# Routed expert tiles with their weights fetched from DRAM as the stationary side, eight exponential buffers, paired weighted sums

## The chip, the cores and the metric

One core of one Trainium2 chip runs the whole program. The metric is device time of one launch in microseconds; where several runs were made, their median counts.

## The reference

The input x has 8 batches of 512 tokens, width 128, float32. Two layers follow each other. In each, for every batch:

```python
h = layernorm(x) * (1 + ca) + sa
x = x + ga * attention(h)          # 16 heads of 8, softmax over 512 keys (causal in layer 1)
h = layernorm(x) * (1 + cb) + sb
x = x + gb * ffn(h)
```

The feed-forward part of layer 0 is a mixture of 8 experts, of which each token takes its best 2, plus a shared expert of width 192; an expert is `(silu(t @ w1) * (t @ w3)) @ w2` with a hidden width of 352. The feed-forward part of layer 1 has 8 experts of width 128 with a squared relu, also with the best 2 per token, and attention there makes q, k and v by way of a latent of 32. The factors sa, ca, ga, sb, cb, gb come from a small product per batch.

## The kernel before, in words

An *item* i is a batch in a layer: items 0 to 7 are layer 0 (`NB` = 8), items 8 to 15 (`N` = 16) layer 1. All matrix work in float32 but the scores (bf16 in three parts) is done as two TensorE instructions per product, which stand as two MATMUL rows in the profile.

**The order of work** is not written by hand. `plan()` (L167) lists some thousands of units of work by `add(engine, key, weight, urgency, after, ...)`, and `Plan.settle` (L92) simulates the five engines with these weights and lags: each engine takes, among the units that can start within `SLACK` (L156) of the earliest, the one of lowest urgency. Urgency is the item's number plus an offset in items, shifted by family in `SHIFT`, and for layer 1 and the last three items in `LATE` and `LAST` (L57 to L61). What comes out is one fixed list per engine (`todo`) and the PSUM banks of each unit. The engines then run their lists in order, each with semaphore waits for what a unit needs. SP's list holds nearly all DMAs, POOL's the indirect ones, so a unit of SP that waits holds up every DMA listed behind it. TensorE has three modes for the plan: "half" (scores, two row halves of the array), "cols" (`pv`, four column groups) and "full" (everything else); a change of mode is given 0.1 us.

**Attention.** For an item and half f of its heads, `score` (L639) makes 128 queries x 512 keys of two heads at a time in two PSUM banks (L647), and `rowmax` (L875) on VectorE takes the maxima; 32 of each per item. The maxima are turned (`max_turn`), split (`max_hi`, `max_lo`), stored to DRAM (`max_st`, L1508) and loaded as three more rows of the query operand (`max_ld`, L1513). `bscore` (L668) then makes keys x queries with the maximum already taken off, `expo` (L1226, ScalarE) writes the exponentials of two heads into one of `NES` = 6 buffers `ES`, and `pv` (L685) sums the values weighted by them: one `pv` per group g of four heads and per key tile j of 128 keys, of four matmuls of 9 columns x 512, one in each column group. A `pv` needs the two `expo` of its j; with six buffers three j are in flight, and `expo` waits for the `pv` of three key tiles before. `u_copy`, `u_st`, `u_ld`, `t_rc`, `t_st`, `t_ld`, `t_o`, `t_mm` (L695) carry the sums through DRAM to the output projection. Each item is begun about one period ahead by `p_norm` (L1161), `p_turn`, `p_ht`, `p_proj` (L630), `p_v`. The buffers `hP` and `lat` are the buffer `xn[0]` (L450), so `p_norm` of an item waits for `p_v` and `p_proj` of the item before.

**Routed experts of layer 0.** For each pair of batches q (items 2q and 2q+1) the 2048 token slots are sorted by expert: `rr_mm`, `rr_a`, `rr_pos`, `rr_tex` find each slot's place and each tile's expert, `r_sc` (L1391, POOL, 16 indirect DMAs, two in flight) scatters rows to `d_h`. There are `NMT` = 23 tiles of 128 rows per pair, 92 in all, and `NXL` = 6 loads of four tiles: `x_ld` (L1564) into the one buffer `hs`, `x_turn` (L743) and `x_hst` make them width x rows in `hsT`. A tile j is then:

- `x_up` (L752), twice: stationary the tile of `hsT` (128 x 128), moving 352 columns of the expert's w1 or w3. All experts' weights lie in SBUF (`f1`, `f3`, `f2`, loaded once); the columns are found by a register, `bass.ds(v, 352)`. Result rows x hidden.
- `x_th` (L1261), `x_gate` (L1061), `x_mul` (L1068): the gated product `hdx`, 128 x 352.
- `x_ht` (L759): three transposes; `x_hc` (L1267): a ScalarE copy to `hxT`.
- `x_dn` (L769): three matmuls of 128 columns, one bank, against rows of `f2` found by a register.
- `x_y` (L1276) and, per four tiles, `x_st` (L1569) to `d_y`.

The registers are loaded on TensorE's own sequencer by `x_reg` (L731), twice per pair, 24 registers each. `x_up` also waits for a `score` of the item that `SPREAD` names, which spaces the tiles out. When a pair's `x_st` are done, `g_ga` (L1414, POOL, indirect) gathers for each 128 tokens two sets of rows into `gr` (four buffers, so a gather waits for the `g_w` of two token tiles before), `g_w` (L1078, L1082) weights them, `g_x` adds them to x. Item 8 + b of layer 1 starts after `g_x` of item b.

**Layer 1's experts** are dense: `d_up` (L777), `d_relu`, `d_sq`, `d_dn` (L784: four matmuls of a new 128 x 128 stationary tile and 128 moving columns each), `d_y`, `d_add` per expert.

Of the kernel before, what the change touches and what calls it, by code (L numbers as in the profile page):

```python
# [17 lines left out]
E = 8  # L18
NG = H // 4
NSTK = 4  # L20
NES = 6
# [35 lines left out]
SHIFT = {"t": -0.39, "s": 1.02, "p": -0.35, "stack": -0.35, "pv": 0.11, "f": 0.37, "d": 1.41, "x": 1.14, "max": -0.38, "r": 0.28, "rr": 0.28, "u": -0.15, "g": -0.54, "bscore": -0.08, "expo": -0.08}  # L57


LATE = {"d": -0.05, "f": -0.22, "score": 0.12, "rowmax": 0.12, "t": 0.43, "max": 0.24, "g": 0.09, "u": 0.82}  # L60
LAST = {"max": -0.08, "r": -0.06, "rr": -0.06, "pv": 0.15}  # L61


class Plan:
# [8 lines left out]
    def add(self, engine, key, weight, urgency, after=(), lag=None, mode="full", opens=0, closes=()):  # L73
# [7 lines left out]
        self.work[key] = (engine, weight, urgency, after, lag, mode, opens, closes)  # L81
# [74 lines left out]
SLACK, SWITCH = 0.05, 0.1  # L156

SPREAD = 2.4, 1.8
# [3 lines left out]
def after_t(i):  # L162

    return ("t_rv" if T_ON_DVE[i] else "t_res", i)


def plan():  # L167
# [17 lines left out]
    for n, name in enumerate(("bo", "c1", "f1s", "f3s", "f2s")):  # L185
# [3 lines left out]
    load("f1", 2.0, 8.0, after=[("score", 2, 0, 0, 0)])  # L189
    load("f3", 2.3, 8.0, after=[("score", 2, 0, 3, 0)])  # L190
    load("f2", 2.6, 8.0, after=[("score", 2, 1, 0, 0)])
# [21 lines left out]
    for i in range(N):  # L213
# [5 lines left out]
        add("ACT", ("p_norm", i), 0.9, i - 0.1, [("p_rstd", i), ("p_turn", i - 1)] + [("p_v", i - 1), ("p_proj", i - 1, 0), ("p_proj", i - 1, 1)])  # L219
        add("PE", ("p_turn", i), 0.45, i, [("p_norm", i), ("c_pool",), ("m_one", l), ("p_v", i - 1), ("p_proj", i - 1, 1), ("p_lat", i - 1)], opens=1)  # L220
        add("ACT", ("p_ht", i), 0.67, i, [("p_turn", i), ("m_one", l), ("p_v", i - 1), ("p_lat", i - 1)], closes=[("p_turn", i)])
        x = ("p_ht", i)
        if not big:
            add("PE", ("p_lat", i), 0.95, i, [("p_ht", i), ("ld", "w1"), ("p_v", i - 1)], opens=1)
            add("ACT", ("p_latc", i), 0.49, i, [("p_lat", i), ("p_v", i - 1)], closes=[("p_lat", i)])
            x = ("p_latc", i)
# [34 lines left out]
        for g in range(NG):  # L261
            f = g // 2
            for j in range(NT):
                u = i + 1.0 + 0.25 * g + 0.0625 * j
                n = S if big else S - 128 * j
                m = NT * (NG * i + g) + j - 3
# [7 lines left out]
                add("PE", ("pv", i, g, j), 0.12 + 0.86 * n / 512, u + 0.06, exps[-2:] + [("p_vs", i)] + ([("pv", i, g, j - 1)] if j else []), mode="cols", opens=int(j == 0))  # L274
# [8 lines left out]
            if i < N - 1 else [("x_up", NB // 2 - 1, NMT - 1, 1)]), lag=4.0)  # L283
# [124 lines left out]
def program(nc, xin, cT, wm, w0, wf1, wf3, wf2, w1, wr1, wr2, bo, out):  # L408
    ctx = ExitStack()
    with ctx:  # L410
# [132 lines left out]
        for n in range(4):  # L543
            s["g_ga", n] = ctx.enter_context(nc.semaphore(f"g_ga{n}"))
# [1100 lines left out]
```

## Time and profile before

| | us |
|---|---|
| median of 3 runs | 1226.88 |
| the runs | 1226.86, 1226.88, 1234.54 |
| the profiled execution | 1231.06 |
| its span, first to last instruction | 1229.0 |

In the rows below, "PE" is TensorE's matmuls, "PEld" its weight loads, "DVE" VectorE, "ACT" ScalarE, "POOL" GpSimd, "SPq" the DMA issues of SP. Times are us unless marked ns; L752 is line 752 of the kernel. On a busy TensorE the distance from one row's start to the next row's start is what the first one cost; the printed duration of a row runs on into the next, since matmuls overlap.

### The profile page before, as it was taken

The numbers are of one execution on the slowest core, as the hardware profiler recorded it, in microseconds if no ns is written. First come the engines' busy times: TensorE is split into PE (matmuls) and PEld (weight loads), VectorE is DVE, ScalarE is ACT, GpSimd is POOL, SyncE is SP. The second block draws the span as 40 slices with busy tenths as digits, with TensorE's granted clock in tenths as the row PEclk, the third lists the DMA queues.
The fourth block names the chain that finished last, engine by engine and source line by source line (L and its number), as shares of the span: only waits on it lengthen the run. The fifth ranks groups of instructions, "written<-read, shape, count | busy, mean of one in ns | idle before, by whom it ended". The sixth has DMA issues, their size and how long they took to land.

```text
span 1229.0 us, 22171 instructions
## 1 busy us (share of the span) xinstructions
PE 1089.1 (89%) x7912; PEld 504.0 (41%) x7912; DVE 879.4 (72%) x1813; ACT 775.3 (63%) x1327; POOL 408.9 (33%) x462
## 2 busy tenths in 40 slices
PE   5588798889999898999989998989998999999985
PEld 3122222123444343444544545545554444544453
DVE  5899788878887676786657776667565777777354
ACT  3058577567766666568765665646766576776853
POOL 2000204250205326314246242351115652433352
PEclk8579898889999898999998999989998899999998
DMA  4705472533316125116144162451512615431110
GB/s 115 167 31 139 175 188 73 138 107 110 101 58 176 50 87 126 62 63 149 60 124 98 36 169 68 112 124 39 132 52 80 149 56 124 113 84 39 55 37 17
DMA packets 120699, 119.36 MB, mean 97 GB/s; under 512 B 17856, under 2 KB 102592, under 8 KB 120208
## 3 DMA queue, kind: packets, MB, share of 16 engines
q1 hardware_dynamic: 115280, 106.68, 32.7%
q0 software_dynamic: 4736, 10.49, 3.0%
q8 instruction: 64, 1.05, 0.4%
q10 hardware_dynamic: 576, 0.79, 0.2%
q14 instruction: 43, 0.35, 0.1%
HBM read 59.26 MB, written 58.62 MB: 96 GB/s over the span
## 4 chain that ended last, share of the span: by engine, by line
PE 47%; DMA 15%; DVE 13%; issue 9%; ACT 8%; POOL 5%; SPq 1%; POOLq 0%; ACTq 0%; DVEq 0%
PE ps L685 9%; PE ps L752 6%; DMA gr<-d_y,pos 6%; DVE nm L875 6%; PE ps L647 5%; PE ps L668 5%; PE ps L769 3%; ACT ES L1226 3%; PE ps L784 3%; DMA d_h<-hx,pos 3%; PE ps L777 2%; ACT xn L1161 2%; PE ps L713 2%; PE ps L759 2%; DMA d_u<-US 2%
## 5 line engine op out<-in xcount | busy, mean ns | idle before, releaser
L875 DVE TENSOR_REDUCE nm<-ps 128x2 f32<-128x1024 f32 (+3 forms) x512 | 508.7, 1018 | 110.9 <-PE ps L653 58.2
L1226 ACT ACTIVATE ES<-ps 128x1024 f32<-128x1024 f32 (+3 forms) x512 | 432.4, 864 | 172.5 <-PE ps L668 94.0
L685 PE MATMUL ps<-ES,VS 128*9 128x512 f32 (+3 forms) x2048 | 237.2, 539 | 1.1 <-DVE nmp L886 0.5
L647 PE MATMUL ps<-KS,QS 48*128 48x512 bf16 (+3 forms) x1024 | 185.6, 369 | 46.8 <-DVE nm L875 26.0
L668 PE MATMUL ps<-QS,KS 51*128 51x512 bf16 (+3 forms) x1024 | 179.9, 355 | 15.1 <-DVE nm L875 5.7
L752 PE MATMUL ps<-f,hsT 128*128 x368 | 142.5, 491 | 5.8 <-DVE nm L875 3.3
L647 PEld LDWEIGHTS ps<-KS,QS 48*128 48x128 bf16 x1024 | 50.5, 95 | 193.6 <-issue 64.3
L668 PEld LDWEIGHTS ps<-QS,KS 51*128 51x128 bf16 x1024 | 49.9, 95 | 177.7 <-issue 73.3
L1434 POOL TENSOR_TENSOR ya<-ya,yS 128x512 f32<-128x512 f32 x49 | 62.2, 1269 | 155.1 <-DVE yS L1121 154.9
L1355 POOL TENSOR_TENSOR sp<-sr,sp 128x512 bf16<-128x512 f32 x32 | 37.1, 1158 | 199.8 <-ACT sp L1202 199.5
L1391 POOL DMA_INDIRECT d_h<-hx,pos x64 | 63.2, 988 | 89.4 <-DMA d_h<-hx,pos 52.1
L1414 POOL DMA_INDIRECT gr<-d_y,pos x64 | 66.6, 1040 | 63.3 <-DMA gr<-d_y,pos 26.1
L769 PE MATMUL ps<-f,hxT 128*128 x552 | 85.5, 292 | 0.9 <-DVE hdx L1061 0.6
L769 PEld LDWEIGHTS ps<-f,hxT 128*128 128x128 f32 x552 | 72.5, 196 | 32.2 <-issue 28.7
L784 PE MATMUL ps<-r,hd 128*128 128x128 f32 x512 | 73.5, 290 | 6.4 <-ACT hd L1298 2.4
L752 PEld LDWEIGHTS ps<-f,hsT 128*128 128x128 f32 x368 | 61.2, 195 | 43.0 <-issue 33.1
L1061 DVE SCALAR_TENSOR_TENSOR hdx<-tx,ps 128x352 f32<-128x352 f32 x92 | 47.2, 514 | 38.4 <-ACT tx L1261 34.6
L784 PEld LDWEIGHTS ps<-r,hd 128*128 128x128 f32 x512 | 64.2, 197 | 24.1 <-ACT hd L1298 13.3
L1290 ACT ACTIVATE tt<-ps 128x512 f32<-128x512 f32 x64 | 38.0, 595 | 45.7 <-PE ps L777 43.7
L777 PE MATMUL ps<-hF,r 128*128 128x512 f32 x112 | 61.7, 634 | 1.9 <-DVE ya L1114 1.7
L1161 ACT ACTIVATE xn<-X,rs 128x128 f32<-128x128 f32 x128 | 52.5, 483 | 16.6 <-POOL rs L1351 16.5
L685 PEld LDWEIGHTS ps<-ES,VS 128*9 128x9 f32 x2048 | 31.3, 89 | 74.4 <-issue 61.0
(190 smaller groups left out, 1471.7 us busy)
## 6 DMA issues: line engine op xcount, KB each, us to landing
d_u<-US SPq DMA_DIRECT2D x64, 256.0 KB
KS<-d_k SPq DMA_DIRECT2D x64, 192.0 KB
QS<-d_q SPq DMA_DIRECT2D x64, 192.0 KB
d_q<-sp SPq DMA_DIRECT2D x16, 384.0 KB
d_k<-sp SPq DMA_DIRECT2D x16, 384.0 KB
hs<-d_h SPq DMA_DIRECT2D x20, 256.0 KB
d_y<-ys SPq DMA_DIRECT2D x20, 256.0 KB, 2.3
d_q<-sp SPq DMA_DIRECT2D x16, 256.0 KB
```

What stands on the lines that cost most here:

```text
L647: mm = eng.matmul(psum[:, bank[u][a], 0:n], QS[m][r:r + KA, pr, 128 * t:128 * t + 128], KS[m][r:r + KA, pr, 0:n], start=True, stop=i < NB)
L668: mm = eng.matmul(psum[:, bank[u][a], 0:S - q0], KS[m][r:r + KB, pr, 128 * j:128 * j + 128], QS[m][r:r + KB, pr, q0:S], start=True, stop=i ...
L685: mm = eng.matmul(psum[32 * a:32 * a + 9, b, q0:S], VS[i % 3][:, j, 4 * g + a, :], ES[(2 * (NT * (NG * i + g) + j) + a // 2) % NES][:, a % ...
L752: eng.matmul(ps(*u)[:, 0:352], T_[:, a0:a0 + 128], (f1, f3)[c][:, bass.ds(v, 352)], start=True, stop=True).then_inc(s["x_up"], 1)
L769: mm = eng.matmul(ps(*u)[:, 0:128], hxT[(NMT * p + j) % 2][0:w, 128 * n:128 * n + 128], f2v[0:w, bass.ds(v + 128 * n, 128)], start=(n == 0 ...
L777: eng.matmul(ps(*u), r1[:, e, :], hFs[i], start=True, stop=True).then_inc(s["d_up"], 1)
L784: mm = eng.matmul(ps(*u)[:, 128 * t:128 * t + 128], hd[e % 2][:, 128 * t:128 * t + 128], r2[:, e, :], start=True, stop=True)
L875: eng.tensor_reduce(nm[f][:, :].rearrange("p (a c) -> p a c", a=2)[:, :, 4 * pr + t], ps2("score", i, f, pr, t)[:, :, 0:n], AX.X, ALU.max, ...
L1161: ins = eng.activation(xn[w][:, t, :], X[:, NT * b + t, :], ACT.Identity, bias=rs[:, w, 2, t:t + 1], scale=rs[:, w, 1, t:t + 1])
L1226: eng.activation(ES[(2 * n + pp) % NES][:, :, 0:S - q0], ps2("bscore", i, f, g, j, pp)[:, :, 0:S - q0], ACT.Exp, scale=SC1 if i >= NB else ...
L1391: eng.indirect_dma_start(out=d_h[p % 2][:, :], out_offset=bass.IndirectOffsetOnAxis(ap=pos[p % 2][:, c, t8:t8 + 1], axis=0), in_=hx[t8 // ...
L1414: eng.indirect_dma_start(out=gr[m][:, :], out_offset=None, in_=d_y[p][:, :], in_offset=bass.IndirectOffsetOnAxis(ap=pos[p % 2][:, c, t8:t8 ...
```

## The change

- `NES` 6 to 8. `pv` units are planned in pairs: at odd j, after the four `expo` of j-1 and j, the `pv` of j-1 and of j are added with one urgency. `expo` waits for the `pv` of four key tiles before.
- The routed weights stay in DRAM as `we`, one block of 128 x 3 x 384 floats per expert (w1, w3 and w2 padded from 352 to 384). A unit of SP, `x_w`, loads one block of 576 KB per tile into one of `NST` = 4 buffers `wst`; it waits for `x_dn` of four tiles before. `x_reg` moves from TensorE to SP and loads 12 registers.
- `x_up` takes 128 columns of the weights as the stationary side, three times per matrix, with the tile of `hsT` as 128 moving columns. Its result is hidden x rows, so `x_ht` and `x_hc` go, `x_th`, `x_gate`, `x_mul` work on 384 columns, and `x_dn` takes `hdx` as it is.
- `hs` gets two buffers, `gr` eight, `hP` and `lat` their own; `f1`, `f2`, `f3` and their loads go, the shared expert has `fs` and one load.
- The last item's private tiles lie in `wst[0]` and `wst[1]` and wait for the last `x_dn` that used these.
- `SHIFT`, `LATE`, `LAST`, `SLACK`, `SPREAD` have other values.

```diff
-NES = 6
+NES = 8
+NST = 4
-SHIFT = {... "d": 1.41, ...}
+SHIFT = {... "d": 1.2, ...}
-LATE = {"d": -0.05, "f": -0.22, "score": 0.12, "rowmax": 0.12, "t": 0.43, "max": 0.24, "g": 0.09, "u": 0.82}
-LAST = {"max": -0.08, "r": -0.06, "rr": -0.06, "pv": 0.15}
+LATE = {... "u": 0.82, "pv": -0.02, "r": -0.23, "rr": -0.23}
+LAST = {"max": -0.08, "r": 0.47, "rr": 0.47, "pv": 0.15, "p": -0.09, "stack": -0.09, "d": 0.41, "u": 0.33, "bscore": 0.11, "expo": 0.11}
-SLACK, SWITCH = 0.05, 0.1
-SPREAD = 2.4, 1.8
+SLACK, SWITCH = 0.01, 0.1
+SPREAD = 2.2, 1.6
...
-                add("PE", ("pv", i, g, j), ..., u + 0.06, exps[-2:] + ..., mode="cols", opens=int(j == 0))
+                for j in (j - 1, j) if j % 2 else ():
+                    n = S if big else S - 128 * j
+                    add("PE", ("pv", i, g, j), ..., u + 0.06, exps[-4:] + ..., mode="cols", opens=int(j == 0))
...
-                        add("PE", ("x_reg", q, h), 2.0, u, [("rr_tex", q), ("x_dn", ...)])
+                        add("SP", ("x_reg", q, h), 1.0, u - 0.35, [("rr_tex", q), ("x_w", ...)], lag=0.1)
...
+                    n = NMT * q + j - NST
+                    add("SP", ("x_w", q, j), 0.5, u - 0.3, [("x_reg", q, h), ("x_dn", n // NMT, n % NMT)], lag=3.6)
-                    add("PE", ("x_ht", q, j), 0.34, ...)
-                    add("ACT", ("x_hc", q, j), 0.37, ...)
...
                 elif k == "x_up":
-                    v = eng.snap(rows[j % 12], min_val=0, max_val=7 * 352)
-                    eng.matmul(ps(*u)[:, 0:352], T_[:, a0:a0 + 128], (f1, f3)[c][:, bass.ds(v, 352)],
-                               start=True, stop=True).then_inc(s["x_up"], 1)
+                    for n in range(3):
+                        mm = eng.matmul(ps(*u)[:, 128 * n:128 * n + 128], wst[(NMT * p + j) % NST][:, c, 128 * n:128 * n + 128],
+                                        T_[:, a0:a0 + 128], start=True, stop=True)
+                    mm.then_inc(s["x_up"], 1)
                 elif k == "x_dn":
-                    for n, w in enumerate((128, 128, 96)):
-                        v = eng.snap(cols[j % 12], min_val=0, max_val=7 * 384)
-                        mm = eng.matmul(ps(*u)[:, 0:128], hxT[...][0:w, 128 * n:128 * n + 128],
-                                        f2v[0:w, bass.ds(v + 128 * n, 128)], start=(n == 0), stop=(n == 2))
+                    for n in range(3):
+                        mm = eng.matmul(ps(*u)[:, 0:128], hdx[...][:, 128 * n:128 * n + 128],
+                                        wst[...][:, 2, 128 * n:128 * n + 128], start=(n == 0), stop=(n == 2))
...
+                elif k == "x_w":
+                    if NMT * p + j >= NST:
+                        q.wait_ge(*on("x_dn", *tile_before(p, j, NST)))
+                    v = eng.snap(tiles[j % 12], min_val=0, max_val=7 * 128)
+                    eng.dma_start(wst[(NMT * p + j) % NST][:, :, :].rearrange("p a b -> p (a b)"),
+                                  we[bass.ds(v, 128), :]).then_inc(slot(*u), 16)
```

## Rows read from the trace of the kernel before

**Rows 1.** The page: the span, and busy time of each engine.
```profile
span 1229.0 us, 22171 instructions
PE 1089.1 (89%) x7912; PEld 504.0 (41%) x7912; DVE 879.4 (72%) x1813; ACT 775.3 (63%) x1327; POOL 408.9 (33%) x462
```

**Rows 2.** Four stretches: length, busy us (count) of each engine, PEclk, DMA share, GB/s.
```profile
60.00:280.00 220.00, 183.07 (x1113) 53.04 (x1111) 185.22 (x312) 149.88 (x198) 56.24 (x67) 0.87 0.43 121
280.00:930.00 650.00, 608.01 (x4366) 300.56 (x4365) 458.02 (x972) 422.73 (x763) 212.96 (x228) 0.97 0.35 94
930.00:1180.00 250.00, 235.51 (x2178) 116.54 (x2177) 169.64 (x395) 171.34 (x310) 111.63 (x112) 0.97 0.33 87
1180.00:1229.00 49.00, 30.50 (x159) 20.91 (x158) 23.90 (x75) 19.04 (x34) 16.48 (x17) 0.90 0.07 22
```

**Rows 3.** Groups by line: busy us, mean ns of one, idle before.
```profile
L752 PE MATMUL ps<-f,hsT 128*128 x368 | 142.5, 491 | 5.8 <-DVE nm L875 3.3 <-DVE sr L868 0.8 <-ACT US L1233 0.5
L769 PEld LDWEIGHTS ps<-f,hxT 128*128 128x128 f32 x552 | 72.5, 196 | 32.2 <-issue 28.7
L1267 ACT ACTIVATE hxT<-ps 128x384 f32<-128x384 f32 x92 | 45.1, 490 | 20.8 <-PE ps L759 20.5
```

**Rows 4.** TensorE in order of time, 572 to 577: start, us, what.
```profile
572.16 0.38 PE L668 MATMUL ps<-QS,KS 51*128 51x512 bf16 x2
572.47 1.04 PE L685 MATMUL ps<-ES,VS 128*9 128x512 f32 x8
573.45 0.39 PE L647 MATMUL ps<-KS,QS 48*128 48x512 bf16 x2
573.77 0.55 PE L759 MATMUL ps<-ident,hdx 128*128 128x128 f32 x3
574.25 0.39 PE L668 MATMUL ps<-QS,KS 51*128 51x512 bf16 x2
574.48 0.38 PE L647 MATMUL ps<-KS,QS 48*128 48x512 bf16 x2
574.79 0.86 PE L752 MATMUL ps<-f,hsT 128*128 x2
575.49 0.83 PE L769 MATMUL ps<-f,hxT 128*128 x6
576.25 0.39 PE L668 MATMUL ps<-QS,KS 51*128 51x512 bf16 x2
```

**Rows 5.** TensorE in order of time: dense experts' L784, eight products in a row.
```profile
1184.82 1.95 PE L784 MATMUL ps<-r,hd 128*128 128x128 f32 x16
1186.61 1.88 PE L777 MATMUL ps<-hF,r 128*128 128x512 f32 x4
```

**Rows 6.** TensorE in order of time: two `pv` in a row.
```profile
510.69 1.90 PE L685 MATMUL ps<-ES,VS 128*9 128x512 f32 x16
512.52 0.39 PE L647 MATMUL ps<-KS,QS 48*128 48x512 bf16 x2
```

**Rows 7.** `pv` alone in 280 to 930: PE busy, PEld busy.
```profile
280.00:930.00 650.00, 118.87 (x1024) 15.83 (x1024) 0.97 0.35 94
```

**Rows 8.** TensorE in order of time: the longest gap released by "issue".
```profile
451.47 0.39 PE L647 MATMUL ps<-KS,QS 48*128 48x512 bf16 x2 [2.06 <-issue]
```

**Rows 9.** Around 124 to 139: SP's issues, the chain that ended last, TensorE.
```profile
123.97 1.06 SPq L1466 DMA_DIRECT2D f<-wf  x2
126.34 7.91 DMA d_m<-nmp
138.80 0.58 PE L695 MATMUL ps<-w0s,OT 128*128 128x128 f32 x1 [4.85 <-DVE OT L897]
```

**Rows 10.** The page's DMA issues: count, KB each, us to landing.
```profile
f<-wf SPq DMA_DIRECT2D x2, 1408.0 KB, 7.3
d_m<-nmp SPq DMA_DIRECT2D x32, 24.0 KB, 1.5
```

**Rows 11.** What SP's queue waited for: us, times, longest.
```profile
SPq L1564 <- PE ps L743: 80.8, 16, 12.9
```

More of the change, by code:

```diff
@@ L80, in add @@
             urgency += LAST.get(family, 0.0)
-        self.work[key] = (engine, weight, urgency, after, lag, mode, opens, closes)
+        self.work[key] = (engine, weight, round(urgency, 3), after, lag, mode, opens, closes)
     @staticmethod
@@ L164, in after_t, with last_in @@
     return ("t_rv" if T_ON_DVE[i] else "t_res", i)
+def last_in(m):
+    n = max(n for n in range(NB // 2 * NMT) if n % NST == m)
+    return n // NMT, n % NMT
 def plan():
@@ L282, in plan @@
         add("SP", ("t_gt", i), 0.5, u - 0.5, [("m_st", l)] + ([("s_x", i - 2), ("r_hx", i - 2), after_t(i - 2), ("d_x", i - 2)]
-            if i < N - 1 else [("x_up", NB // 2 - 1, NMT - 1, 1)]), lag=4.0)
+            if i < N - 1 else [("x_dn", *last_in(0))]), lag=4.0)
         add("DVE", ("t_o", i), 0.61, u, [("t_ld", i)])
@@ L334, in plan @@
                     if j % 12 == 0:
-                        add("PE", ("x_reg", q, h), 2.0, u, [("rr_tex", q), ("x_dn", q - (h == 0), NMT - 1 if h == 0 else 11)])
+                        add("SP", ("x_reg", q, h), 1.0, u - 0.35, [("rr_tex", q), ("x_w", q - (h == 0), NMT - 1 if h == 0 else 11)], lag=0.1)
                     L = j // 4
@@ L376, in plan @@
             u = i + 2.35
-            add("DVE", ("d_comb", i), 0.43, u, [("f_idx", i), ("d_y", i - 2, E - 1) if i < N - 1 else ("x_dn", NB // 2 - 1, NMT - 1)])
+            add("DVE", ("d_comb", i), 0.43, u, [("f_idx", i), ("d_y", i - 2, E - 1) if i < N - 1 else ("x_dn", *last_in(1))])
             for e in range(E):
@@ L456, in program @@
         hx = [sb(f"hx{i}", [128, NT, D]) for i in range(2)]
-        hs = sb("hs", [128, 4, D])
+        hs = [sb(f"hs{i}", [128, 4, D]) for i in range(2)]
         ys = [sb(f"ys{i}", [128, 4, D]) for i in range(2)]
@@ L460, in program @@
         cv = sb("cv", [128, NT, D])
-        gr = [sb(f"gr{i}", [128, D]) for i in range(4)]
+        gr = [sb(f"gr{i}", [128, D]) for i in range(8)]
         ohs = sb("ohs", [128, 2, 8, E])
@@ L579, in _ @@
             q = Queue(eng)
-            rows, cols = ([eng.alloc_register(f"row{k}_{n}") for n in range(12)] for k in range(2))
-            f2v = f2[:, :, :].rearrange("p a b -> p (a b)")
             def open_banks(u):
@@ L1059, in _ @@
                     if p or j > 1:
-                        q.wait_ge(*on("x_ht", *tile_before(p, j, 2)))
-                    eng.scalar_tensor_tensor(out=hdx[m][:, :], in0=tx[m][:, :], scalar=1.0, in1=ps("x_up", p, j, 0)[:, 0:352],
+                        q.wait_ge(*on("x_dn", *tile_before(p, j, 2)))
+                    eng.scalar_tensor_tensor(out=hdx[m][:, :], in0=tx[m][:, :], scalar=1.0, in1=ps("x_up", p, j, 0)[:, 0:384],
                                              op0=ALU.add, op1=ALU.mult).then_inc(s[k], 1)
@@ L1151, in _ @@
                         q.wait_ge(*on(("p_turn", "f_turn")[w], i - 1))
-                    if w == 0 and i:
-                        q.wait_ge(*on("p_v", i - 1))
-                        for n in range(2):
-                            q.wait_ge(*on("p_proj", i - 1, n))
                     if w == 1 and 0 < i <= NB:
@@ L1534, in _ @@
                     if i == N - 1:
-                        q.wait_ge(*on("x_up", NB // 2 - 1, NMT - 1, 1))
+                        q.wait_ge(*on("x_dn", *last_in(0)))
                     elif i >= 2:
```

205 lines of the change are left out of this document (91 added, 114 removed).

## The prediction

> **What bounds the kernel now.** I read the page first, then busy time by stretch, then the groups by line, and last TensorE in order of time. The page gives TensorE 1089.1 of 1229.0 us, VectorE 879.4, ScalarE 775.3 [rows 1]. The stretches show that this share is not one thing [rows 2]. From 60 to 280 us, where no expert tile runs, VectorE (185.2 of 220) and TensorE (183.1, at a granted clock of 0.87) are equally full and neither sets the pace alone. From 280 to 930, where all 92 tiles lie, TensorE is busy 608.0 of 650 us (93.5%) at 0.97 of its clock, VectorE 70%, ScalarE 65%: TensorE is the bound there, and only 42 us are left over. From 930 to 1180 it is the same (235.5 of 250). The last 49 us are one item's chain, where TensorE works 30.5 us. DMA is busy 35% in the middle stretch and is not a bound, but it is what the change loads most.
>
> So the sum goes by TensorE's time from 280 to 1180, and I ask of each edit what it takes from TensorE's list there.
>
> **Tiles with the weights as the stationary side.** A busy TensorE's cost is the distance between starts. An `x_up` costs 575.49 - 574.79 = 0.70 us [rows 4], the three transposes of `x_ht` 0.48, `x_dn` 0.76. A tile before is 2 x 0.70 + 0.48 + 0.76 = 2.64 us. Afterwards `x_up` is three products of a new 128 x 128 stationary tile and 128 moving columns, which is the form of `x_dn`: 0.76. A tile is 3 x 0.76 = 2.28. The check is the dense experts' L784, of the same form, eight products in 1.79 us or 0.224 each [rows 5]; three of them and one entry of 0.09 make 0.76. The saving is 0.36 x 92 = 33 us. Units that stand directly behind each other save the entry already, so it can be less (0.24 a tile, 22 us); a visit less between two scores saves another 0.09 (rows 4: `bscore` costs 0.23 ahead of a score, 0.31 ahead of other work), at most 41. I take 30.
>
> A rule speaks against this part. The rows first: a weight load of this form lasts 0.196 us [rows 3], and a tile goes from 13 loads (4 for `x_up`, 3, 6) to 18. Rows 5 hold 16 loads, some 3.1 us of them, in 1.79 us, so they lie beside the matmuls. The Trainium skill, page "TensorE: Matmul & The Clock Gate", section "Part 3: Packing small matmuls — row/col tiling", says that a weight load overlaps running matmuls only where the row group differs, and here it is the same; by it the added loads would be exposed. The rows contradict that for this form. What exposure would cost is a rival below.
>
> **What else leaves the tile.** `x_hc` is 45.1 us of ScalarE [rows 3]; wider `x_th`, `x_gate`, `x_mul` (384 for 352 columns) give back some 3 us on ScalarE and 7 us on VectorE, neither of them the bound. The tile's own chain is shorter by about a microsecond, which matters only to the gathers behind it. I count nothing. Bounds: 7 us lost if VectorE were the bound, 5 gained.
>
> **`x_reg` to SP.** TensorE's sequencer loads 24 registers eight times. It shows as a gap released by "issue", the longest 2.06 us [rows 8]. 8 x 2.06 = 16 us; where TensorE waits anyway it is free. I take 13. On SP it is 12 loads, beside DMAs that mostly wait for something else.
>
> **Pairs of `pv`.** A lone `pv` costs 0.98 us and makes the score ahead of it 0.31 instead of 0.23 [rows 4]. Two in a row cost 1.83 [rows 6]. A merge saves 2 x 0.98 - 1.83 + 0.08 = 0.21 us. 128 of the 256 `pv` lie in the middle stretch (1024 matmuls, eight each) [rows 7]: 64 merges, 13 us, less the few that are merged already. The other 64 merges are worth another 13, half of them before 280, where TensorE isn't alone. I take 12 + 8 = 20. The wait it adds: a `pv` of an even j stands behind two more `expo`; scores and tiles of other items are queued around it, and eight buffers keep two pairs in flight, one filled while one is summed. If ScalarE then had to wait for the pair, every pair could lose up to one `expo`, 1.02 us; I see no reason in a stretch where ScalarE is 65% busy, and take nothing (bound: 10 us lost).
>
> **The loads of f1, f2, f3 go.** At 123.97 two of them are issued, 1408 KB each, and the small store of the maxima at 126.34 lands 7.91 us later instead of 1.5; TensorE then stands 4.85 us [rows 9, 10]. This gap goes: 5 us. Next is whatever VectorE and TensorE share there.
>
> **The weight blocks, `x_w`.** 92 blocks of 576 KB. In rows 9 the store behind 2816 KB came 6.4 us late, so those 2816 KB were through about 8.8 us after their issue: 1.8 us a block. That is 166 us of all DMA engines, 27% of the stretch on top of 35%. A block is wanted every 6.5 to 7 us and four are in flight, so the tile itself will rarely wait. The price is paid by others: whatever stands behind a block in SP's queue comes up to 1.8 us late, on average 0.27 x 0.9 = 0.25 us if blocks and others mix at random. Some 8 transfers in a row carry one item's attention (store of q and k, stack, maxima out and in, sums out and in, reciprocals out and in), nine items in the stretch: 72 x 0.25 = 18 us, and a third of it seen, 6 us. Lower end 0, upper end is the rival below.
>
> **SP's list.** `x_w` and `x_reg` also put 100 units into SP's in-order list, and each `x_w` waits for an `x_dn`. Behind it stand the stores of the maxima and sums, for which `bscore` and `t_mm` wait. Against this the two `hs` buffers take away most of the 80.8 us that SP stood for `x_turn` in 16 waits, up to 12.9 us long [rows 11]. I set these against each other, zero, between 15 gained and 30 lost.
>
> **Small edits.** Own `hP` and `lat`, eight `gr`: waits on work long done, or off the path, 0 to 4 us, taken as 0. The new offsets: those for `r` and `rr` in `LATE` and `LAST` touch nothing, since these units exist for items 0 to 7 alone; the rest reorders layer 1 and the last three items. `SPREAD` ends the tiles 0.4 of an item earlier. No row prices an order; TensorE's idle time after 930 is 14.5 + 18.5 us [rows 2], so I allow 12 either way and take 0.
>
> **Sum.** 30 + 13 + 20 + 5 = 68 us off TensorE's list. Not all of it becomes time: in the middle TensorE's 93.5% goes to some 91%, because waits for VectorE, ScalarE and DMA don't shrink with it. I count 0.7 of it, 48, less 6 for contention: 42 us. The profiled execution was 1231.06 (span 1229.0 and 2.1 around it), 4.2 above the median of the runs; I take the difference from the median: 1226.9 - 42 = 1185 us.
>
> **Rivals.**
> - *The whole of it and more*: TensorE takes all 68 us, and the earlier tiles and the new order add some 8. 1227 - 76 = 1151 us. For it: 93.5% busy over 650 us. Against it: the waits named. Chance 0.2.
> - *Another engine or a latency is the bound already*: the freed time of TensorE turns into waiting for VectorE's maxima and for the chain through DRAM. 1227, plus or minus 10. For it: the stretch before 280 is shared [rows 2], and 185 of 220 for VectorE is no slack. Against it: 458 of 650 for VectorE in the middle. Chance 0.13.
> - *The blocks delay everything behind them* (the slower side): each of the 72 transfers stands behind one whole block, 1.8 us, and 4.85 of 6.4 us of delay reach TensorE, as in rows 9: 72 x 1.8 x 0.76 = 98 us, against 48: 1277 us. It decides from a mean delay of 48 / (72 x 0.76) = 0.9 us a transfer, half a block. For it: one queue carries nearly all DMAs, and blocks are freed in bursts as the tiles run. Against it: the plan knows of one unit per block and keeps four buffers. Chance 0.12.
> - *Weight loads exposed*: 5 x 0.196 x 92 = 90 us against 48: 1269 us. Rows 5 speak against it. It is what the rule named above would give. Chance 0.03.
> - That a merge doesn't happen is hardly possible, since both `pv` become ready together with one urgency; if half of them are split, 10 us are lost, inside the forecast's range.
>
> **How the numbers follow.** My forecast, 1185 with its own range of 1167 to 1205, has 0.52. A measurement of this kernel tells about 1% from no change. Faster by over 1% holds the forecast and the first rival, 0.72; within 1%, 0.13; slower, 0.15. The range goes from 1148 to 1250: it leaves out part of the first rival and most of the two slow ones.
>
> **What would show it.** Right: L759 and L1267 gone; L752 as 1104 rows of the form and mean of L769 (0.275 us), about 1.4 us a tile; `pv` in runs of 16; TensorE's time from the first to the last tile down from 650 to some 605 us and its share still above 0.9; DMA share in that stretch near 0.6; landing of the small stores below 3 us. Wrong: TensorE's share below 0.88 there with VectorE or "DMA d_m", "DMA QS", "DMA DR" as releasers (contention), SP waiting long on L769 with maxima behind it, or starts of L784 and L752 more than 0.3 us apart (exposed loads). If the first item's stretch before 280 doesn't shorten at all, that takes some 8 us from my sum.

## The result and the profile after

The changed kernel takes 1249.5 us (median of 4 runs, 1244.5 to 1252.9), beside 1227.9 us for the kernel before on the same chip (4 runs, 1226.9 to 1234.5): a ratio of 1.0156, 95% interval 1.0121 to 1.0191. It is 22 us slower, where the forecast was 42 us faster. The profiled execution took 1252.24 us, with a span of 1250.5.

Busy times from the page of the changed kernel, then busy times by stretch (length, busy us and count of each engine, PEclk, DMA share, GB/s):

```profile
span 1250.5 us, 22791 instructions
PE 1068.2 (85%) x8372; PEld 548.1 (44%) x8372; DVE 882.0 (71%) x1809; ACT 742.8 (59%) x1235; POOL 409.3 (33%) x462
```

```profile
60.00:280.00 220.00, 181.79 (x1128) 52.22 (x1128) 188.20 (x321) 152.37 (x201) 56.47 (x67) 0.90 0.43 115
280.00:960.00 680.00, 599.88 (x4819) 352.16 (x4819) 456.82 (x971) 390.74 (x674) 218.78 (x235) 0.93 0.58 166
960.00:1200.00 240.00, 225.26 (x2149) 109.93 (x2147) 169.82 (x383) 167.07 (x301) 103.44 (x103) 0.99 0.33 87
```

TensorE's busy time fell, but by much less than the 68 us of the forecast: 1089.1 to 1068.2 us, by 20.9 [rows 1]. Its idle time grew by twice that: 1229.0 - 1089.1 = 139.9 us before, 1250.5 - 1068.2 = 182.3 after. Nearly all of this growth, 38 of 42 us, lies in the stretch of the tiles: TensorE is busy 88% there and was at 93.5%, the granted clock is 0.93 and was 0.97, and the DMA share is 0.58 where it was 0.35 [rows 2]. The first tile starts at 283 us, 6 us later than before. From there to the end of the last tile it takes 682 us, where it took 653 and 605 were forecast. What follows the last tile is 13 us shorter.

The groups by line (busy us, mean ns of one, idle before and its releasers), the tile's two products and their weight loads:

```profile
L750 PE MATMUL ps<-hsT,wst 128*128 128x128 f32 x1104 | 162.9, 294 | 6.6 <-DVE hdx L1048 2.7 <-DVE nm L864 1.9 <-DVE hd L964 1.1
L750 PEld LDWEIGHTS ps<-hsT,wst 128*128 128x128 f32 x1104 | 142.8, 202 | 41.5 <-issue 31.7 <-DVE hdx L1048 4.8 <-DVE nm L864 2.0
L758 PE MATMUL ps<-wst,hdx 128*128 128x128 f32 x552 | 87.5, 297 | 13.0 <-DVE hdx L1055 12.6 <-ACT US L1219 0.4
```

And of the kernel before the two that stood beside L752 of [rows 3]:

```profile
L769 PE MATMUL ps<-f,hxT 128*128 x552 | 85.5, 292 | 0.9 <-DVE hdx L1061 0.6
L759 PE MATMUL ps<-ident,hdx 128*128 128x128 f32 (+1 forms) x276 | 49.2, 288 | 3.4 <-DVE hdx L1068 3.3
```

The tiles cost 142.5 + 49.2 + 85.5 = 277.2 us before and 162.9 + 87.5 = 250.4 after. 27 us are gone, and the loads of the stationary side (142.8 us of them for `x_up`) lie beside the products. The whole of TensorE agrees: busy time times the mean granted clock, a measure of the work that doesn't move with the clock, is 1089.1 x 0.933 = 1016 us before and 1068.2 x 0.926 = 989 after, 27 less. So only the tiles' part of the forecast shows in TensorE's work (`x_reg` and the loads of f were gaps), and a lower clock gives back 6 us of it.

Where the waits are, from the profile's list of waits (engine, line, releaser: total us, times, longest):

```profile
POOL d_h L1371 <- DMA d_h<-hx,pos: 71.0, 25, 7.4
POOL gr L1394 <- DMA gr<-d_y,pos: 50.1, 22, 5.4
PE ps L651 <- DVE nm L864: 44.0, 39, 9.0
PE ps L672 <- DVE nm L864: 23.2, 21, 5.6
PE ps L672 <- ACT ES L1212: 16.0, 9, 13.0
DVE DC L881 <- DMA OT<-d_u: 33.2, 9, 11.0
ACT xn L1144 <- POOL rs L1331: 30.0, 14, 13.4
```

and the same of the kernel before:

```profile
POOL d_h L1391 <- DMA d_h<-hx,pos: 52.1, 26, 5.5
POOL gr L1414 <- DMA gr<-d_y,pos: 26.1, 17, 3.4
PE ps L647 <- DVE nm L875: 26.0, 34, 3.0
PE ps L668 <- DVE nm L875: 5.7, 13, 1.3
ACT xn L1161 <- POOL rs L1351: 16.5, 11, 3.8
```

The waits for DMA rose on GpSimd, and each engine's wait for the next rose behind it. One case in full, in order of time (start, us, what, idle before and releaser), is TensorE's longest gap:

```profile
405.07 0.97 POOL L1371 DMA_INDIRECT d_h<-hx,pos  x1 [3.40 <-DMA d_h<-hx,pos]
408.57 0.97 POOL L1371 DMA_INDIRECT d_h<-hx,pos  x1 [1.25 <-DMA d_h<-hx,pos]
410.89 0.23 POOL L1326 TENSOR_SCALAR rs<-mv 128x4 f32<-128x4 f32 x1
412.86 1.65 ACT L1144 ACTIVATE xn<-X,rs 128x128 f32<-128x128 f32 x4 [13.43 <-POOL rs L1331]
414.41 1.00 ACT L1212 ACTIVATE ES<-ps 128x1024 f32<-128x1024 f32 x1
415.47 0.61 PE L672 MATMUL ps<-QS,KS 51*128 51x512 bf16 x2 [12.96 <-ACT ES L1212]
```

GpSimd scatters rows to DRAM, two transfers in flight, and each next one waits for the landing of the one two before. `rs`, four short operations of the next item's norm, stands in its list behind them; six are issued while ScalarE waits. ScalarE's `p_norm` waits for `rs` for 13.4 us, an `expo` stands behind `p_norm`, and TensorE stands 13 us for the `expo`.

### The profile page after: what moved, and what is told of

It reads as the page before. It is cut to its first block, busy times and chain, and to the rows that moved or that the text cites. A ratio compares the mean times of both kernels' runs of the same rounds, so it can differ in the third digit from the quotient of the medians.

```text
span 1250.5 us, 22791 instructions
## 1 busy us (share of the span) xinstructions
PE 1068.2 (85%) x8372; PEld 548.1 (44%) x8372; DVE 882.0 (71%) x1809; ACT 742.8 (59%) x1235; POOL 409.3 (33%) x462
## 4 chain that ended last, share of the span: by engine, by line
PE 34%; DMA 22%; issue 14%; DVE 13%; POOL 8%; ACT 6%; SPq 1%; POOLq 0%; DVEq 0%; ACTq 0%
DMA d_h<-hx,pos 9%; DMA gr<-d_y,pos 8%; PE ps L689 7%; DVE nm L864 6%; PE ps L750 5%; PE ps L672 4%; PE ps L651 3%; PE ps L758 3%; PE ps L773 3%; ACT xn L1144 2%; POOL gr L1394 2%; ACT ES L1212 2%; PE ps L766 2%; POOL d_h L1371 2%; PE ps L717 1%
## 5 line engine op out<-in xcount | busy, mean ns | idle before, releaser
L864 DVE TENSOR_REDUCE nm<-ps 128x2 f32<-128x1024 f32 (+3 forms) x512 | 507.2, 1016 | 109.8 <-PE ps L657 57.3
L689 PE MATMUL ps<-ES,VS 128*9 128x512 f32 (+3 forms) x2048 | 237.8, 539 | 0.3 <-DVE rj L990 0.2
L750 PE MATMUL ps<-hsT,wst 128*128 128x128 f32 x1104 | 162.9, 294 | 6.6 <-DVE hdx L1048 2.7
L750 PEld LDWEIGHTS ps<-hsT,wst 128*128 128x128 f32 x1104 | 142.8, 202 | 41.5 <-issue 31.7
L758 PE MATMUL ps<-wst,hdx 128*128 128x128 f32 x552 | 87.5, 297 | 13.0 <-DVE hdx L1055 12.6
L758 PEld LDWEIGHTS ps<-wst,hdx 128*128 128x128 f32 x552 | 72.8, 200 | 33.9 <-DVE hdx L1055 16.1
L1048 DVE SCALAR_TENSOR_TENSOR hdx<-tx,ps 128x384 f32<-128x384 f32 x92 | 50.3, 546 | 34.3 <-ACT tx L1247 33.9
L773 PEld LDWEIGHTS ps<-r,hd 128*128 128x128 f32 x512 | 61.6, 191 | 24.2 <-ACT hd L1278 14.5
L1247 ACT ACTIVATE tx<-ps 128x384 f32<-128x384 f32 x92 | 45.2, 491 | 37.3 <-PE ps L750 31.2
L689 PEld LDWEIGHTS ps<-ES,VS 128*9 128x9 f32 x2048 | 31.0, 89 | 69.1 <-issue 58.9
```

The source lines that it names most:

```text
L689: mm = eng.matmul(psum[32 * a:32 * a + 9, b, q0:S], VS[i % 3][:, j, 4 * g + a, :], ES[(2 * (NT * (NG * i + g) + j) + a // 2) % NES][:, a % ...
L750: mm = eng.matmul(ps(*u)[:, 128 * n:128 * n + 128], wst[(NMT * p + j) % NST][:, c, 128 * n:128 * n + 128], T_[:, a0:a0 + 128], start=True, ...
L758: mm = eng.matmul(ps(*u)[:, 0:128], hdx[(NMT * p + j) % 2][:, 128 * n:128 * n + 128], wst[(NMT * p + j) % NST][:, 2, 128 * n:128 * n + 128 ...
L773: mm = eng.matmul(ps(*u)[:, 128 * t:128 * t + 128], hd[e % 2][:, 128 * t:128 * t + 128], r2[:, e, :], start=True, stop=True)
L864: eng.tensor_reduce(nm[f][:, :].rearrange("p (a c) -> p a c", a=2)[:, :, 4 * pr + t], ps2("score", i, f, pr, t)[:, :, 0:n], AX.X, ALU.max, ...
```

## The experiments

Theory A: the weight blocks (576 KB each, 54 MB in all) make other transfers land late, and this is what costs. Theory B: the new order of the lists costs. Theory C: the pairs of `pv` cost. All ratios are to the kernel before, with 95% intervals.

**The blocks without most of their bytes.** Every engine's list stays as it is. 88 of the 92 blocks bring 64 KB in place of 576, 46 of the 54 MB are gone, and the later tiles compute with what stood in their buffers:

```diff
-                    eng.dma_start(wst[...], we[bass.ds(v, 128), :])
+                    cut = 3 * 384 if NMT * p + j < NST else 128
+                    eng.dma_start(wst[...][:, 0:cut], we[bass.ds(v, 128), 0:cut])
```

> The kernel after the change, every list and wait as it is; only the first four weight blocks are loaded whole, the other 88 bring 128 of 1152 columns (64 instead of 576 KB), so later tiles compute with stale weights. Theory 1 (the bytes of the blocks lengthen the serial indirect DMAs, 16 scatters from 34.3 us to 39.8 and 16 gathers from 36.9 to 41.0 on average, and POOL, VectorE, SP and ScalarE stand behind them in their fixed lists): the chains go back to under 37 us, TensorE's gaps of 5 to 13 us go, and the time falls by 20 us or more, to 1229 or less. Theory 2 (the new order of the lists itself, with SP's waits for x_dn, costs the time): within 6 us of the 1249.5 of the changed kernel.

1206.1 us (0.9805, 0.9751 to 0.9859). The bytes cost 1249.5 - 1206.1 = 43 us, and without them the change would gain 21. SyncE's time for the 92 issues is not part of it: about 34 us in both traces. The gap of 12.96 us shown above is 7.8 us here.

**The kernel before with the traffic alone**: 92 transfers of 576 KB from DRAM to DRAM, issued from SyncE between the first `x_ld` and the last `x_st` of each pair of items; nobody waits for them.

```diff
+                for n in extra.get(u, ()):
+                    eng.dma_start(d_s[n], wx).then_inc(more, 16)
```

> The kernel before, its lists untouched, with 92 more DMAs in SP's list that nobody waits for: 576 KB each, 23 of them spaced evenly over the units from a pair's first x_ld to its last x_st, from DRAM to DRAM in rows of 4608 bytes. It keeps the old tiles, six buffers and the old constants. Theory 1 (bytes beside the indirect DMAs): slower than before by 20 us or more, 1248 and up, with TensorE's gaps of several us before work that a late scatter or gather holds up. Theory 2 (the order of the lists): within 8 us of 1228, since SP's issue of 92 DMAs is some 35 us in a queue that mostly waits.

1280.8 us (1.041, 1.0352 to 1.0468): 53 us for 54 MB that are read and also written to DRAM. Two kernels with unlike lists pay a price of the same size. This run alone doesn't part the bytes from the 92 issues, which take SyncE some 0.51 us each; the run before does.

**The pairs of `pv` made one unit.** A `pv` is eight MATMUL instructions. In TensorE's order of time, 246 rows of L689 hold eight and only 5 hold sixteen (238 and 9 in the kernel before): the planner did not put the two of a pair one behind the other. Here it must:

```diff
-                for j in (j - 1, j) if j % 2 else ():
-                    n = S if big else S - 128 * j
+                if j % 2:
+                    n = 2 * S if big else 2 * (S - 128 * j) + 128
```

> The kernel after the change, with the pv of two key tiles as one unit of the plan, so that they stand directly behind each other; in the changed kernel they don't (226 pieces of 8 matmuls in the trace, 5 of 16), because the second of a pair is given the lag of 0.48 us behind the first. The rest as changed. If a merge saves the 0.21 us that I worked out, some 110 merges take up to 23 us from TensorE's list, and 10 to 18 of them come out: 1232 to 1240. Rival (TensorE isn't the bound any more where its gaps come from late DMAs): within 8 us of 1249.5. In either case pieces of 16 matmuls in the trace and TensorE's busy time down by some 10 us or more.

1277.1 us (1.0395, 1.0331 to 1.0459), 28 us slower still, though all 128 rows are now as I had wanted them:

```profile
442.58 1.90 PE L692 MATMUL ps<-ES,VS 128*9 128x512 f32 x16
447.75 1.90 PE L692 MATMUL ps<-ES,VS 128*9 128x512 f32 x16
```

The `pv` rows fell from 237.8 to 214.2 us. But TensorE's busy time rose from 1068.2 to 1076.8, where 10 us less were expected: the granted clock is 0.908 and was 0.926. While a pair runs, no score and no expert product is made. ScalarE's waits for TensorE, here and in the changed kernel:

```profile
ACT ys L1259 <- PE ps L761: 62.3, 37, 10.4
ACT US L1222 <- PE ps L692: 44.6, 34, 6.6
```

```profile
ACT ys L1256 <- PE ps L758: 42.3, 40, 6.8
ACT US L1219 <- PE ps L689: 28.0, 23, 10.6
```

**What the planner believes of a scatter.** Its weight of 1.28 and lag (its landing time behind the issue) of 2.1 give 3.38 us from one scatter to the one two behind it, so 25 us from the first to the last of sixteen. The traces show 30.8 to 37.6 us from the first to the last of sixteen before, 34.9 to 44.1 after. With small blocks and the same lists they take 33.3 to 36.0. So units that a real scatter delays are planned close behind it. The lag is the same in both kernels, and I raise it in both:

```diff
-  add("POOL", ("r_sc", q, t, c), 1.28, u, [...], lag=2.1)
+  add("POOL", ("r_sc", q, t, c), 1.28, u, [...], lag=4.0)
-  add("POOL", ("g_ga", i0, t, k), 1.28, u, [...], lag=2.1)
+  add("POOL", ("g_ga", i0, t, k), 1.28, u, [...], lag=4.0)
```

> The kernel after the change, with one thing told to the plan: the indirect DMAs r_sc and g_ga land 4.0 us after their issue instead of 2.1, which makes a chain of 16 about 42 us in the plan as it is on the chip. Work is the same, the lists are laid out anew. Theory 1 (late scatters and gathers hold up what stands behind them): the rows behind them move ahead, TensorE's gaps over 4 us in the middle stretch (56 us in seven gaps in the changed kernel) fall below half, and the time to 1215 to 1238. Theory 2 (gaps have another cause): within 8 us of 1249.5. A new layout alone may move the time by some us either way.

> The kernel before with the one edit of e5: the plan is told that the indirect DMAs land after 4.0 us instead of 2.1. Tiles, weights in SBUF, buffers and constants as before. If the 42 us that e5 took from the changed kernel was the repair of what the weight traffic had broken (the before kernel's chains last 34 to 37 us against 27 in its plan, the changed kernel's 40 to 41), this one gains little, 1215 to 1232, and the changed kernel with the true lag is the faster of the two. Rival (the lag is an old fault of the plan that has nothing to do with the change): as large a gain here, 1185 to 1200, and the change costs its 20 us with either lag.

> e5 (changed kernel, lag 4.0) with the blocks of e1 (88 of 92 cut to 64 KB, so later tiles compute with stale weights). With the old lag the bytes cost 43 us (1249.5 against 1206.1). If they cost time only by way of units that come later than the plan had them, little is left: 1195 to 1205 against 1207.5. If the bytes cost time however the lists are laid out: 1165 to 1180.

| us (ratio to before) | kernel before | change, 64 KB blocks | change, whole blocks | the bytes |
|---|---|---|---|---|
| lag 2.1 | 1227.4 (1) | 1206.1 (0.9805) | 1249.5 (1.0156) | 43.4 |
| lag 4.0 | 1202.5 (0.9787) | 1164.8 (0.9494) | 1207.5 (0.9822) | 42.7 |

The bytes cost 43 us in either row. The lag is worth 25 us to the kernel before and 42 to the changed one. With it the change costs 5 us, not 22. Its other parts together gain 21 us by the old lag and 38 by the new. The kernel before gained more than I had expected of it, and the change did not come out ahead. Of the kernels that do the whole work, the kernel before with a lag of 4.0 has the lowest median, 2.1% below the kernel before (0.974 to 0.9833).

With equal lists the two traces of the last row can be laid side by side, instruction by instruction. Their spans differ by 1208.9 - 1160.2 = 48.7 us: 16.3 of them are TensorE's busy time (1061.9 against 1045.6), 32.4 are idle. The busy part is the clock: the products are the same, and 1061.9 x 0.940 and 1045.6 x 0.955 are both 998 us. By stretch, first with whole blocks, then with small ones:

```profile
280.00:960.00 680.00, 627.33 (x5167) 362.67 (x5159) 493.97 (x1035) 415.02 (x720) 242.24 (x257) 0.96 0.62 175
```

```profile
280.00:960.00 680.00, 652.22 (x5548) 375.62 (x5548) 528.67 (x1127) 444.82 (x778) 268.63 (x287) 0.99 0.43 114
```

From 280 to 960 the distance between the same instruction of TensorE in both grows from 4.2 to 47.9 us, and 12 steps of over 1 us make 32 us of that. The largest, 5.5 us, is this one. The chain that ended last (start, us, what), then SyncE, VectorE and TensorE in order of time, whole blocks:

```profile
723.67 9.00 DMA d_u<-US
733.32 3.82 DMA OT<-d_u
```

```profile
718.00 3.21 SPq L1553 DMA_DIRECT2D wst<-we  x2
723.67 0.33 SPq L1496 DMA_DIRECT2D d_u<-US  x1
732.74 0.54 SPq L1504 DMA_DIRECT2D DC<-d_u  x1
737.16 0.55 DVE L881 RECIPROCAL DC<-DC 128x64 f32<-128x64 f32 x1 [6.62 <-DMA OT<-d_u]
737.63 0.49 DVE L1055 TENSOR_TENSOR hdx<-ps,hdx 128x384 f32<-128x384 f32 x1
738.18 1.65 PE L758 MATMUL ps<-wst,hdx 128*128 128x128 f32 x6 [6.09 <-DVE hdx L1055]
```

The last store of the sums takes 9.0 us. With small blocks the same step (store issued, then the issue of the load that waits for it) is this:

```profile
689.12 0.33 SPq L1496 DMA_DIRECT2D d_u<-US  x1
692.90 0.54 SPq L1504 DMA_DIRECT2D DC<-d_u  x1
```

3.8 us, and TensorE waits 0.55 us there. `t_rc` stands in VectorE's list, the tile's `x_mul` (L1055) stands right behind it, and TensorE stands for `x_mul`. The plan gives the store 2.4 us to land (the lag of `u_st`); the late landing opens the gap.

**Pairs planned as units, with the lag of 4.0** (the two edits above together).

> e3 (the two pv of a pair as one unit of the plan, 1277) with the lag 4.0. Mode changes of TensorE stay near 820 against 1028. If merging was bad only since more hung on late DMAs, it now shows its 0.21 us a pair: 1185 to 1203, faster than e5's 1207.5. Rival (a unit of 1.85 us that needs four exponentials makes ScalarE and the scores wait for each other, whatever the lag): slower than e5, 1215 to 1240.

1243.8 us (1.0116, 1.007 to 1.0161), 36 us above the changed kernel with the lag alone.

**Six buffers and single `pv`** as before, all else as changed.

> The changed kernel with six exponential buffers and each pv planned by itself as before; tiles, weight blocks, other buffers and constants as changed, lag 2.1. The change's pairs were not merged in the trace, so what is left of this part is looser waits and a later even pv. I expect no clear difference, 1240 to 1258. If the eight buffers and the paired planning cost the time (pv later, scores held up), it is faster by 10 us or more, below 1239.

1255.7 us (1.0208, 1.0157 to 1.0259), 6 us above the changed kernel. The intervals overlap, so this doesn't show that the eight buffers with their grouped planning are worth anything.

**The old constants of the planner** (`SHIFT`, `LATE`, `LAST`, `SLACK`, `SPREAD`) in the changed kernel.

> The changed kernel with the planner's constants of the kernel before (the shifts of due times, the slack and the spread of the tiles over the key tiles). If the new constants were set for the new order and carry part of its time, this is slower than 1249.5 by over 5 us; if constants don't matter at this size it is within 5 us of it. A time under 1240 would say that part of the loss comes from the new constants.

1276.5 us (1.0373, 1.0344 to 1.0402). The new constants carry 27 us of the changed kernel's time. They hide part of what the change costs. Whether they are worth as much with small blocks or the new lag was not run.

**Which way do the bytes go? First, round trips.** The waits that keep two scatters and two gathers in flight are taken away. In the first three kernels the planner's dependency goes too, so the lists are new; in the last two they are those of the lag of 4.0.

```diff
-                    if t8:
-                        q.wait_ge(s["r_sc", p % 2, c], 128 * (p // 2) + 16 * t8)
-                    if n:
-                        q.wait_ge(s["g_ga", 2 * ((n - 1) % 4) + c], 16 * ((n - 1) // 4 + 1))
```

> The changed kernel with the honest lag of 4.0, and the sixteen indirect scatters of a pair of items issued without waiting for the one two before them, the gathers likewise (they wait for their data and their buffer alone). Theory: the weight blocks cost time mostly because each of them stretches the round trips of indirect transfers of which only two are in flight, so that GpSimd's list and everything behind it waits. Then a chain of scatters falls from about 42 us to under 30, and the kernel from 1207 to about 1180. Rival: the blocks cost what they cost by bandwidth (every transfer lands later, chains or not); then the chain is shorter but the time stays within 10 us of 1207.

> The same with 88 of the 92 weight blocks cut from 576 to 64 KB, which leaves the later blocks' weights as they were in their buffers, so the product of those tiles is not the right one. Theory (round trips): the distance to the run with whole blocks is under 20 us, where it was 43 with chains of two. Rival (bandwidth): it is again about 40 us, and this run comes out near 1150 to 1165.

> The kernel before with the same lag of 4.0 and the same unchained scatters and gathers (it has four gather buffers in place of eight). It moves its routed weights inside SBUF-resident tiles and had little waiting behind the chains: 1202 with the lag alone. Theory (round trips): it gains little, 1190 to 1202, so that the changed kernel comes out ahead of it. Rival: it gains as much as the changed kernel, and stays ahead by about 5 us.

1249.6 us (1.0163, 1.0115 to 1.021), 1214.4 (0.9875, 0.9845 to 0.9904) and 1246.5 (1.0128, 1.0097 to 1.0159). Both theories failed: without the chain the three kernels are 42, 50 and 44 us slower than with it. The bytes still cost 35.

> The changed kernel with the honest lag of 4.0, all engines' lists as they are there, and only the waits taken away that keep two scatters, and two gathers, in flight (the lists were replanned in the earlier run with free chains, so that it mixed two edits). If the chain of round trips is what carries the blocks' delay to TensorE: about 1190 to 1200 against 1207.5. If not: within 5 us of 1207.5.

> The same with the small blocks (88 of 92 cut to 64 KB, their products not the right ones). By round trips the distance to the run with whole blocks falls from 43 us to under 25; otherwise it stays at 35 to 45, and this run is near 1165.

1241.2 us (1.0116, 1.0071 to 1.0161) and 1222.8 (0.9946, 0.9922 to 0.9969). With the same lists it is slower by 34 and by 58 us; the bytes cost 18. Two of the four runs of sixteen scatters now take 22.0 and 20.6 us in both kernels, instead of 33 to 43, and while they are issued the other engines stand. The small-block kernel, GpSimd, then TensorE and ScalarE in order of time:

```profile
715.63 0.97 POOL L1369 DMA_INDIRECT d_h<-hx,pos  x1 [0.30 <-issue]
716.91 0.97 POOL L1369 DMA_INDIRECT d_h<-hx,pos  x1 [0.30 <-issue]
```

```profile
710.96 1.60 PE L750 MATMUL ps<-hsT,wst 128*128 128x128 f32 x12
712.13 0.60 ACT L1212 ACTIVATE ES<-ps 128x512 f32<-128x512 f32 x1 [0.63 <-PE ps L677]
717.96 0.49 ACT L1247 ACTIVATE tx<-ps 128x384 f32<-128x384 f32 x1 [5.23 <-remote]
721.48 0.60 ACT L1212 ACTIVATE ES<-ps 128x512 f32<-128x512 f32 x1 [3.04 <-remote]
```

So this pair does not measure the round trips' share: it brings in a new stall. What share of the 43 us passes through the chains stays open.

**Second, the queue.** The blocks and the tile numbers go from SyncE's list to ScalarE's, which feeds another hardware queue:

```diff
-  add("SP", ("x_w", q, j), 0.5, u - 0.3, [...], lag=3.6)
+  add("ACT", ("x_w", q, j), 0.5, u - 0.3, [...], lag=3.6)
```

> The changed kernel with the honest lag of 4.0, and the reading of the tile numbers and the issues of the weight blocks moved from SyncE's queue to ScalarE's. Theory (a queue's order): the small exchanges that the critical chain goes through (sums stored and read back, row maxima, scattered rows) stand behind one or two blocks of 576 KB on the queue that SyncE feeds, 3.2 us a block at the 180 GB/s of the trace; with a queue of their own the blocks no longer stand ahead of them. ScalarE pays some 0.45 us an issue, 41 us in all, beside work. Expected 1185 to 1200, against 1207.5. Rival (shared bandwidth): the same 16 DMA engines carry both queues, so the exchanges land as late as before; 1207 or, with ScalarE's added work, up to 1225.

> The same with 88 of the 92 blocks cut from 576 to 64 KB (those tiles' products use what was in the buffers). The distance to the run with whole blocks is the price of the bytes when they have their own queue: under 20 us by the queue's order, again 35 to 45 by shared bandwidth.

1217.8 us (0.9923, 0.9887 to 0.9959) and 1177.0 (0.9589, 0.9548 to 0.9629). The distance is 41 us, as with one queue. The whole is 10 to 12 us slower; I put that down to the 92 issues in ScalarE's list, which no run shows by itself. That a transfer stands behind a block in its own queue is thus not the way. The chain that ended last has a store of the sums that takes 11.2 us although no block was issued on its queue:

```profile
715.97 11.19 DMA d_u<-US
```

In the small-block kernel of this pair the same step takes 4.5 us (the store is issued at 693.37, the load that waits for it at 697.91).

The Trainium skill, page "DMA: Bandwidth & Descriptors", section "Queues, rings and completion order", says that each DMA engine serves its queues in turn, a packet at a time. By that alone a small store would pass a block; the runs show no gain. The same section says that a transfer's completion signal lands only after all earlier writes of that DMA engine, in whatever queue they were. The 41 us agree with this, and as well with a plain sharing of the DMA engines by both queues, the rival on record for this run; no run here shows the signal apart from the data.

**Two checks on the size of chance.** The lag at 5.0 in the changed kernel, and the slack alone (0.05 to 0.01) in the kernel before:

> The changed kernel with the lag of scatters and gathers at 5.0 in place of 4.0 (2.1 as it came). Under the whole blocks a pair of scatters takes 39 to 45 us over eight, so some 5 us each. If the planner still believes in too short a round trip, this gains 5 to 15 more and lands near 1195, below the kernel before with its lag of 4.0 (1202.5). If what was left is not the list's order but transfers that land late whatever the order, within 8 us of 1207.5.

> The kernel before with the planner's slack at 0.01 in place of 0.05, the smallest of the changed constants, and nothing else. It measures how far an edit of the order alone moves the time: expected within 10 us of 1228. A larger distance says that differences of this size between two kernels with other lists are not to be read as the price of an edit.

1212.2 us (0.9821, 0.9743 to 0.9899) and 1227.6 (0.996, 0.9929 to 0.9991). The ratio at 5.0 is that at 4.0, so no more is to be had from the lag. Here a new order alone moved 0.4%; I don't read differences below some 6 us between unequal lists, and the 5 us between the two kernels with a lag of 4.0 are among these. But the lag, too, is a new order alone, and it moved 25 and 42 us. So the prices of the bytes (43, 43 and 41 us) are the firm ones, since each stands between equal lists. The price of the merged pairs stands between unequal lists; it came twice, 28 and 36 us, and its cause is not isolated.

Of the theories at the start, A holds. B does not by itself: with the changed kernel's own lists and small blocks the time is below that of the kernel before. C does not either: the pairs weren't merged, and single `pv` with six buffers gained nothing.

Weights resident in SBUF as the stationary side, chosen by a register, would have parted the form of the product from the traffic. It wasn't tried.

## Why the prediction was wrong

**The step that failed** is the price of the blocks: "I count 0.7 of it, 48, less 6 for contention". The bytes cost 43 us in place of 6, by a direct removal under two lags; a direct addition to the other kernel cost 53. What the blocks take of the DMA engines was right: 166 us forecast, 0.58 x 680 - 0.35 x 650 = 167 measured. What this does to others was wrong. I worked it out from a mean delay, 0.27 x 0.9 = 0.25 us a transfer. But the lists are in fixed order and planned by one landing time each, and the price sits mostly in a few places: 12 steps make 32 of 44 us, and in the largest, the one traced here, a store takes 9.0 us beside 3.8. Nor did I count the granted clock, which is 0.96 in the stretch with whole blocks, where TensorE stands more, and 0.99 with small ones. That is a third of the loss, 16 of 49 us. The rival "the blocks delay everything behind them" had the right cause and the right engines. Its price (98 us) was too high, and its path, SyncE's queue, was not it: 41 us remain when the blocks have their own. By which path the delay passes, landing signals or shared DMA engines, stays open.

**A second step failed, the sum of TensorE's list**: 68 us forecast, 34 by the sizes below. By the forecast's own working, 0.7 of 34 less 6, it would have made a gain of 42 into one of 18, and not into a loss.

**GpSimd's chains were missing from the steps.** I named eight transfers in a row for the attention, and not the thirty-two indirect ones of a pair of items, whose landings pace GpSimd's list. A lag that was too short in both kernels made this 17 us worse in the changed one (42 against 25). That is most of the difference between slower and even.

**Tiles**: right. 30 us forecast, 27 in the groups by line. The rival of exposed weight loads is out: 142.8 us of loads lie beside 162.9 us of products.

**`x_reg`**: mis-sized. I multiplied the longest gap by eight. The list of waits gives all of TensorE's gaps released by "issue" as 2.1, 1.9, 0.6 and 0.2 us before and 0.4 and 0.3 after: 4 us, not 13. The row that groups them was there to be read.

**The loads of f**: the gap is right, its worth isn't shown. The gap of 4.85 us before L695 [rows 9] is now one of 1.39 before L699 (the same unit), 3.5 us off, of 5. But the stretch before 280 did not get shorter, which I had named as a sign that would take 8 us from the sum: TensorE's busy time from 60 to 280 is 181.79 us and was 183.07, and the first tile came 6 us later.

**Pairs of `pv`**: wrong twice. "Hardly possible" that they don't merge: the plan gives the second a dependency on the first with TensorE's lag of 0.48, and fills that time with a score. And 0.21 us saved per merge is not there to be had: forced, the pairs save 23.6 us in the `pv` rows, TensorE's busy time grows all the same by 8.6 us, and the kernel loses 28 and 36 us. The likely cause is that a block of 1.90 us on TensorE delays the scores that VectorE and ScalarE live on, which I had bounded at 10 us. The longer waits of ScalarE agree with it; a new order of the lists came along with it, so it isn't shown.

**The constants**: mis-sized. I took 0 and allowed 12 us either way; they are worth 27 us in the changed kernel.

**The sum**: by these sizes it is 27 + 4 + 3.5 = 34 us off TensorE's list, 27 by the measure of busy time and clock. Without the bytes the change gains 21 (lag 2.1) or 38 us (lag 4.0). That the forecast's working comes out near these is luck in part: they hold the constants, for which the sum had nothing. The factor of 0.7 can't be checked. What turns a gain of 21 us into a loss of 22 is the bytes alone.

## What to carry to other kernels

Price added traffic by its latest landings and not by their mean: find each in-order list that holds a DMA wait, ask what stands right behind it, and take the landing time behind one or two whole blocks, in any queue. Before judging a change of a planned kernel, compare the planner's lags with the trace's landings, since a wrong lag taxes two versions unequally. A group's total in the list of waits is the bound of a gap's cost, not its longest times a count, and a switch saved on TensorE can be worth nothing: here a longer unit made the kernel slower under both lags.

## What the hardware showed that was not expected

In the two kernels with unchained scatters in the old order, other engines stand for 3 to 9 us at a time while indirect scatters are issued back to back (0.97 us each, 0.30 between). The list of waits names no releaser of this core for these, and such rows stand in no other trace. With small blocks:

```profile
DVE nm L864 <- remote: 34.5, 10, 5.6
ACT ys L1256 <- remote: 22.1, 5, 7.3
ACT ES L1212 <- remote: 18.4, 9, 3.8
ACT tx L1247 <- remote: 15.2, 4, 5.2
```

In the rows shown above, `x_th` at 717.96 reads products of L750 whose row ends at 712.56. So what comes late, as far as these rows tell, is TensorE's signal to ScalarE and not the landing of a DMA. Back-to-back scatters alone don't explain it. The unchained kernel with new lists issues all sixteen at the same pace, in 19.3 us, has no such wait, and TensorE stays busy. A run of scatters in that kernel, then one in the small-block kernel of the old order:

```profile
549.00:568.50 19.50, 19.41 (x154) 10.39 (x150) 15.35 (x21) 13.10 (x21) 14.93 (x16) 1.00 0.55 175
```

```profile
705.00:726.00 21.00, 9.13 (x99) 6.37 (x99) 8.56 (x18) 6.05 (x11) 16.29 (x18) 0.79 0.45 149
```

What sets off the late signals, these runs don't show. Keeping two in flight, which looked like a cost, was faster in all five pairs of kernels, by 34 to 58 us; these stalls can be the reason in two of them at most. The other surprise is that a second hardware queue took nothing off the price of the blocks: 41 us against 43.
